# Layer 3's capped mixture: where the fallback, the second biases and the first experts' results are computed

## The reference, cut to what matters

```
probs = softmax(xf @ Wr);  scores, experts = top_k(probs, 2);  scores /= sum
y_fb = gelu(xf @ fw1 + fb1) @ fw2 + fb2          # the fallback, for tokens that overflow
for e in range(8):
    eligible = (token chose e) & ~fb_mask
    rank = cumsum(eligible) - 1
    keep = eligible & (rank < CAP);  overflow = eligible & ~keep
    fb_mask |= overflow
    y = where(overflow, y_fb, y)
    h = gelu(xf[kept tokens] @ W1[e] + b1[e])
    y_e = h @ W2[e] + b2[e]
    y[kept tokens] += y_e * weight
```

## Time and profile before

| | |
|---|---|
| median of 3 runs | 2565.21 us (2561.59 to 2570.26) |
| the profiled execution | 2564.71 us |
| its span | 2562.9 us |
| busy over the span: PE, DVE, ACT, POOL | 78%, 60%, 51%, 19% |
| the last stage | from about 2391 us to the end |

### The profile page before, as it was taken

One profiled execution on the slowest core, in us unless ns is written; L12 is line 12 of the kernel. 1 busy time (PEld: TensorE's weight loads), 2 busy tenths in 40 slices (PEclk: granted clock), 3 DMA queues, 4 the chain that ended last, 5 costly groups with the idle time before them and its releaser, 6 DMA issues.

```text
span 2562.9 us, 40084 instructions
## 1 busy us (share of the span) xinstructions
PE 1999.9 (78%) x14307; PEld 1353.0 (53%) x14307; DVE 1543.1 (60%) x3577; ACT 1306.1 (51%) x2677; POOL 490.2 (19%) x531
## 2 busy tenths in 40 slices
PE   6999757879999999567760678999998984488646
PEld 4666643447777777323440445566665773234435
DVE  6787676756666666457469545666664561478412
ACT  4666434657777776236642146666663120256412
POOL 2111021114232323131025321000100000221133
PEclk9999977989999999769885789999998995689868
DMA  4000004310000000043010000000001010132212
GB/s 172 1 1 2 1 13 90 80 34 1 1 1 1 1 1 1 9 88 86 1 68 0 0 9 1 1 1 1 1 1 77 1 37 13 37 87 60 66 36 68
DMA packets 83302, 73.90 MB, mean 29 GB/s; under 512 B 8633, under 2 KB 76361, under 8 KB 82081
## 3 DMA queue, kind: packets, MB, share of 16 engines
q1 hardware_dynamic: 81313, 68.95, 9.7%
q0 software_dynamic: 1792, 2.38, 0.3%
HBM read 54.73 MB, written 17.62 MB: 28 GB/s over the span
## 4 chain that ended last, share of the span: by engine, by line
PE 49%; DVE 22%; issue 8%; SPq 7%; ACT 7%; another core or an unknown queue 4%; DMA 3%; POOL 1%; DVEq 0%; ACTq 0%; POOLq 0%
PE bank L468 42%; SPq L1408 7%; DMA scratch<-parts 2%; DVE w_keep L1921 1%; PE bank L652 1%; PE bank L2868 1%; PE bank L368 1%; DVE scratch L1225 1%; ACT w_early L3109 1%; PE bank L692 1%; DVE stats L245 1%; DVE w_early L2532 1%; DVE scratch L3007 1%; DVE scratch L720 1%
## 5 line engine op out<-in xcount | busy, mean ns | idle before, releaser
L468 PE MATMUL bank<-scratch 64*128 64x256 bf16 (+5 forms) x3664 | 395.9, 321 | 122.4 <-DMA scratch<-parts 81.7
L468 PEld LDWEIGHTS bank<-scratch 64*128 64x128 bf16 (+3 forms) x3664 | 220.4, 123 | 268.4 <-issue 80.9
L1225 DVE TENSOR_REDUCE scratch<-bank 128x2 f32<-128x512 f32 x384 | 245.9, 687 | 128.1 <-PE bank L468 125.6
L468 PE MATMUL bank<-w_keep,scratch 128*128 128x128 f32 (+4 forms) x1760 | 246.5, 332 | 35.4 <-ACT scratch L805 20.8
L1311 ACT ACTIVATE w_keep<-bank 128x512 f32<-128x512 f32 x384 | 210.4, 596 | 94.9 <-PE bank L468 89.3
L468 PE MATMUL bank<-XNT,w_keep 128*128 128x256 f32 (+4 forms) x800 | 237.6, 436 | 7.2 <-POOL w_keep L2169 2.5
L468 PEld LDWEIGHTS bank<-w_keep,scratch 128*128 128x128 f32 (+3 forms) x1760 | 183.9, 185 | 97.0 <-issue 45.9
L468 PE MATMUL bank<-w_early,scratch 128*128 128x128 f32 (+4 forms) x1184 | 170.8, 350 | 40.2 <-DVE X L3388 24.9
L3109 ACT ACTIVATE w_early<-bank,scratch 128x256 f32<-128x256 f32 x256 | 123.7, 564 | 131.0 <-DVE scratch L3011 131.0
L468 PEld LDWEIGHTS bank<-XNT,w_keep 128*128 128x128 f32 x800 | 149.0, 196 | 60.9 <-issue 29.4
L468 PEld LDWEIGHTS bank<-w_early,scratch 128*128 128x128 f32 (+4 forms) x1184 | 127.6, 191 | 96.4 <-issue 69.0
(11 more groups left out here) (438 smaller groups left out, 3762.9 us busy)
## 6 DMA issues: line engine op xcount, KB each, us to landing
scratch<-parts SPq DMA_DIRECT2D x768, 32.0 KB
parts<-scratch SPq DMA_DIRECT2D x24, 384.0 KB, 2.8
w_early<-pack_l3f SPq DMA_DIRECT2D x1, 4758.0 KB, 14.8
w_keep<-pack_l2f SPq DMA_DIRECT2D x1, 2124.0 KB, 13.3
w_early<-pack_mamba SPq DMA_DIRECT2D x1, 2120.0 KB, 19.1
w_keep<-pack_l2x SPq DMA_DIRECT2D x1, 2049.0 KB, 8.7
w_keep<-taps SPq DMA_DIRECT2D x4, 512.0 KB, 5.4
w_keep<-wave_kernels SPq DMA_DIRECT2D x1, 2048.0 KB
```

The lines of the kernel that those rows point to most:

```text
L468: return pe.matmul(out, lhsT, rhs, start=start, stop=stop, skip_group_check=True)
L1225: dve.tensor_reduce(neg[:, :, h], self.k.bank[5 - g % 2][:, :].rearrange("p (t s) -> p t s", s=S), AXX, ALU.max, negate=True).then_inc(*s. ...
```

## The change: what it does

- The second biases of the experts are packed as rows for all partitions (`z_b2`, 8 x 128 columns), and the instruction that copied an expert's result from the bank now adds its row. `biases_pe`, `turned_act` and `biases_dve` are no longer called in this stage.
- The fallback's bias becomes a product of one row (ones times the bias) in the same bank, a fifth product for each tile; the 16 DVE instructions of L3663 go.
- The second products of fallback jobs 0 and 1 are cut into four pieces each, one behind each expert's rank products. Jobs 2 and 3 follow right behind the ranks: both first products, then both second ones. ACT's order follows.
- DVE's fallback sums move behind the results of experts 1 to 4.
- The semaphore of results is split: experts 0 to 6, and expert 7. SP fetches all of the first half once 0 to 6 are written, then the second half once 7 is; DVE adds all four quarters of the first half, then those of the second.

The diff, without the declarations of the semaphores and the packing:

```diff
@@ def cap_pe(pe):
+        pieces = [piece for job in range(2) for piece in [fallback_down_pe(pe, job)] * 4]
         for e in range(E8):
...
             mm(pe, bank[:, 0:NT], after, el, False, True).then_inc(*s.projected.up("rank", e))
+            next(pieces[e])
@@ def fallback_down_pe(pe, job):
         for j in range(4):
+            o = bank[:, j * P:(j + 1) * P]
             for c in range(C):
-                m = mm(pe, bank[:, j * P:(j + 1) * P], hidden[job % 2][:, c * BANK + j * P:c * BANK + (j + 1) * P],
-                       w["z_fw2"][:, c * D:(c + 1) * D], c == 0, c == C - 1)
-        m.then_inc(*s.summed.up("down", job))
+                mm(pe, o, hidden[job % 2][:, c * BANK + j * P:c * BANK + (j + 1) * P], w["z_fw2"][:, c * D:(c + 1) * D], c == 0, False)
+            m = mm(pe, o, w["ones"][0:1, :], w["z_fb2_bc"][0:1, :], False, True)
+            if j == 3:
+                m.then_inc(*s.summed.up("down", job))
+            yield
@@ def pe(e):
         cap_pe(e)
-        fallback_down_pe(e, 0)
-        fallback_down_pe(e, 1)
-        core.biases_pe(e)
+        core.up_pe(e, 2)
+        core.up_pe(e, 3)
         for job in (2, 3):
-            core.up_pe(e, job)
-            fallback_down_pe(e, job)
+            for _ in fallback_down_pe(e, job):
+                pass
         slots_pe(e, 0)
@@ def result_dve(dve, e):
-        dve.tensor_copy(ys[e], k.bank[6 + e % 2][:, 0:SLOTS]).then_inc(*s.divided.up("expert", e))
+        dve.tensor_tensor(ys[e].rearrange("p (b d) -> p b d", d=D), k.bank[6 + e % 2][:, 0:SLOTS].rearrange("p (b d) -> p b d", d=D),
+                          b2(e).unsqueeze(1).to_broadcast([P, 3, D]), ALU.add).then_inc(*s.divided.up("expert", e))
@@ def dve(e):
         shares_dve(e)
-        core.biases_dve(e)
-        fallback_dve(e)
         turned_dve_(e, 0)
...
             result_dve(e, n)
+            if n <= QUARTERS:
+                fallback_dve(e, n - 1)
         e.wait_ge(*s.vector.at("share", 1, "sum"))
-        for q in range(QUARTERS):
-            for n in range(2):
...
+        for n in range(2):
+            for q in range(QUARTERS):
+                result_sums_dve(e, n, q)
@@ def act(e):
         lower_act(e, 1)
-        core.turned_act(e)
         for job in (2, 3):
             core.raise_act(e, job)
+        for job in (2, 3):
             lower_act(e, job)
@@ def sync(e):
-        e.wait_ge(*s.results_out.at("block", E8 - 1, len(BLOCKS) - 1))
-        for q in range(QUARTERS):
-            for n in range(2):
+        for n in range(2):
+            e.wait_ge(*s.results_out[n].at("block", E8 - 2 + n, len(BLOCKS) - 1))
+            for q in range(QUARTERS):
```

More of the change, by code:

```diff
@@ L3258, in __init__ @@
         self.order, self.top = tmp(k, E8), tmp(k, NT)
-        self.wt = tmp(k, T)
+        self.wt = tmp(k, T) if b2 is not None else None
     def on_dve(self, c):
@@ L3499, in capped_mixture @@
     fallback = [(w["z_fw1"], w["z_fb1"], w["z_fw2"], None)]
-    core = Mixture(k, fallback, MOE3_H, ACT.Gelu, w["z_wr"], w["z_b2"], ALU.max, 1, True)
+    core = Mixture(k, fallback, MOE3_H, ACT.Gelu, w["z_wr"], None, ALU.max, 1, True)
     hidden = core.hidden
@@ L3549, in slots_pe @@
         pe.wait_ge(*s.slots_in[e].at("rows"))
-        pe.wait_ge(*(s.flip_v.at("slots", e - 2) if e >= 2 else s.added.at("b2", e + 2)))
+        pe.wait_ge(*(s.flip_v.at("slots", e - 2) if e >= 2 else s.vector.at("rank", E8 - 1)))
         for b, (at, n) in enumerate(BLOCKS):
@@ L3658, in shares_dve, with fallback_dve, result_sums_dve @@
             dve.tensor_reduce(share[n], same, AXX, ALU.add).then_inc(*up("sum"))
[L3660 to L3665, removed]
-        for q in range(QUARTERS):
-            dve.wait_ge(*s.lowered.at("fallback", q))
-            for i in range(4 * q, 4 * q + 4):
-                o = dve.scalar_tensor_tensor(out=k.X[:, i, :], in0=away[:, i, :], scalar=lost[:, i:i + 1], in1=k.X[:, i, :], op0=ALU.mult, op1=ALU.add)
-            o.then_inc(*s.added.up("fallback", q))
+    def fallback_dve(dve, q):
+        dve.wait_ge(*s.lowered.at("fallback", q))
+        for i in range(4 * q, 4 * q + 4):
+            o = dve.scalar_tensor_tensor(out=k.X[:, i, :], in0=away[:, i, :], scalar=lost[:, i:i + 1], in1=k.X[:, i, :], op0=ALU.mult, op1=ALU.add)
+        o.then_inc(*s.added.up("fallback", q))
+    def result_sums_dve(dve, n, q):
+        dve.wait_ge(*s.fetched_in[n][q].at("rows"))
+        dve.wait_ge(*(s.added.at("result", 0, q) if n else s.added.at("fallback", q)))
+        for i in range(4 * q, 4 * q + 4):
+            o = dve.scalar_tensor_tensor(out=k.X[:, i, :], in0=fetched[n][:, i, :], scalar=share[n][:, i:i + 1], in1=k.X[:, i, :],
+                                         op0=ALU.mult, op1=ALU.add)
+        o.then_inc(*s.added.up("result", n, q))
     def turned_dve_(dve, e):
@@ L4156 @@
     vals.update(z_wr=g[a + "Wr"], z_w1=g[a + "W1"].transpose(1, 0, 2).reshape(P, -1), z_b1=col(g[a + "b1"].ravel()),
-                z_w2=np.concatenate([chunks(w) for w in g[a + "W2"]], 1), z_b2=g[a + "b2"], z_fw1=g[a + "fw1"],
+                z_w2=np.concatenate([chunks(w) for w in g[a + "W2"]], 1), z_b2=rep(g[a + "b2"].ravel()), z_fw1=g[a + "fw1"],
                 z_fb1=col(g[a + "fb1"]), z_fw2=chunks(g[a + "fw2"]), z_fb2_bc=rep(g[a + "fb2"]))
```

16 lines of the change are left out of this document (5 added, 11 removed).

## The result

The changed kernel takes 2547.85 us (median of 10 runs, 2538.43 to 2559.52), the kernel before 2565.18 beside it (10 runs, 2556.31 to 2570.26): ratio 0.9937, 95% interval 0.9914 to 0.9959. The forecast of 2534 was too low by 13.9 us, and 2547 was the upper end of its range. Of the predicted 31.1 us the two profiled executions show 20.2 (2564.71 to 2544.55).

A forecast was written before the change was run, and what follows sets the result against it. The prediction took fallback and bias products to hold up expert 1 some 30 us after POOL delivered its rows. 28.1 us there plus 3 in the tail made 31.1 off 2564.7: 2533.6, median 2534, range 2528 to 2547.

The forecast's parts named there:

- the one on expert 0: Expert 0, 8.4 us long, ends at 2461, hidden 10 us ahead of expert 1's rows.
- the late release stays and takes expert 0: Rival, chance 0.22: under POOL's token writes DVE gets expert 0's turned slots late; +1 to +7 us, forecast 2540.
- the cold clock's 1.7: Expert 1's eight products on PE take 4.11 us, not 2.42, after idling: 1.7 us off the gain.
- The rank loop: Pieces between PE's rank products lengthen the period from 1.13 to 1.29 us; POOL's first token write 1.1 us later.
- the rival of the lower clock: Rival, chance 0.10: PE's ranks run at the lower clock, costing 10.9 us for 1.1; 2544.
- Jobs 2 and 3: These fallback jobs follow the ranks, take 17 us, end at about 2441, hidden under POOL's writes with 10 us spare.
- The tail: Final sums: first results fetched and added ahead; 3.8 us by the steps, bounds 0 to 4.7, taken as 3.
- the sharing: In the final fetches, early fetch and POOL's last rows delay each other; one us less for it.
- The addition in the copy: DVE's copy of each expert's result also adds the second bias: +0, between -0.1 and +0.13 us each.
- The slower rival: Rival, chance 0.04: POOL's indirect writes stall the new additions in experts 1 to 7's results; +57 us, 2590.
- The weighed rule: DVE's fallback sums, with two SBUF inputs, could be held up to 3.8 us each by POOL's result writes; 2535.
- the middle of the change: Expert 1's first product starts 29.8 us earlier, at 2472.3 for 2502.08; 28.1 us left after the clock term.

The follow-up runs named there:

- before_again: The kernel before, unchanged, profiled anew on chip 11: 2542.0 us.
- bias_on_dve: Changed kernel without the one-row products, the fallback's bias again as 16 DVE instructions ahead of the first slots: 2548.86 us (one run).
- half_writes: Changed kernel without POOL's second 16 token writes, SP waiting for the first 16 alone: 2531.85 us (one run).
- half_third: Changed kernel without POOL's second 16 token writes, on chip 6: 2528.33 us (one run).
- half_again: Changed kernel without POOL's second 16 token writes, on chip 5: 2521.1 us (one run).
- wide_pack: Kernel before with the second biases' part of the pack 896 columns wider, never read, on chip 10: 2568.74 us, ratio 1.002.
- lean_again: Changed kernel with fallback jobs 0 and 1 uncut behind the ranks and the fallback's bias as 16 DVE instructions, chip 10: 2554.27 us (one run).
- tail_only: Kernel before with only the results' semaphore split and the first half fetched and added ahead: 2534.53 us, ratio 0.999.
- after_again: The changed kernel, unchanged, run again on chip 11: 2545.55 us, ratio to before 1.001.

## Why the prediction was wrong

*The step that failed is the one on expert 0* ("hidden too, 10 us ahead of expert 1's rows"). It took PE's handoffs during POOL's token writes to be prompt once the bias products are gone. The rival "the late release stays and takes expert 0" describes what happened, down to the place: release at 2475.13 with SP's seven reads (2471.70 on), expert 0 from 2475.18 to the first product of expert 1 at 2484.82. It was priced at +1 to +7; with SP's seven reads from 2471.70, 3.6 to landing and 1.1 for turning, that product could have started at 2476.4, so it came 8.4 late, less the cold clock's 1.7 that expert 0 pays again: 6.7 us. The evidence for it stood in the earlier trace rows: an engine other than DVE, with a finished bank, late in that same stretch. I gave the rival 0.22 because the handoffs of the earlier trace rows behind 2502 were prompt; those stand beside bursts of three writes and not beside 32 in a row.

*A reading of the earlier trace rows* was wrong besides: engines do work in the first of its two pieces. PE goes on there, with gaps, until its first bias products end at 2440.8, 15.2 of the 28.00 us, and POOL writes all along; what idles is DVE. The late release is the other 12.8, and part of the 15.2 is the hold too: these products end 16.4 us behind POOL's first write here and 9.4 in `before_again`.

*The rank loop*: predicted 1.29 us a period, measured 1.55. POOL's first write is 3.0 us later for it, not 1.1: 2.7 in the loop itself, the rest between the logits and the first rank product. The clock was 1.00, as forecast, and the rival of the lower clock did not come. The mis-sized term is the one-row product, costed at 0.24 like two full records and measured at 0.41; by `bias_on_dve` the eight others cost nothing.

*The logits* were 2.3 us later behind the stage's start (13.3 for 11.0; the clock of the stretch behind them is 0.81 for the 1.00 of the earlier trace rows). `half_writes` and `half_third` have it, `half_again`, the same kernel, doesn't, and `wide_pack` has it with before's order: scatter, which no step had.

The three make 6.7 + 1.9 + 2.3 = 10.9, less 0.2 by which the tail was better than forecast: 10.7 of the 10.9 us missing in the profiles (31.1 - 20.2). The other 3 us between the forecast and the median are the profiled run's distance from it (2544.55 to 2547.85).

*Jobs 2 and 3* were to be over by 2441; PE was dense until 2443.7 and then held to 2467. The second product of job 2 took 5.9 us (2434.82 to 2440.72) and not 4.8, again by the one-row products. Neither cost anything by itself: in `lean_again` PE had turned the slots by 2469.1, and DVE got them at 2485.21, behind the writes all the same.

*The tail*: 3.0 forecast, 3.2 measured in the pair and in `tail_only`. It was less than the 3.8 of the steps, and the reason given, the sharing, fits: the second fetch is issued 3.2 us behind the last write's end (2529.48 to 2532.65), 1.24 before, and DVE idles 1.26 us between the halves.

*The addition in the copy*: +0, and 0.56 us like the copy. The slower rival is out: no result waited for POOL. What came late was DVE's plain copy of the slots, and ACT's copies.

*The weighed rule* (two SBUF inputs on DVE are blocked by a GpSimd instruction that reads SBUF): beside POOL's result writes four fallback sums took 1.13 us, as they did alone (1.14 in before). So DVE was not held, as the weighed reading had it; it was POOL: the first write beside them took 1.12 us and not 0.97, and in `before_again` a token write beside the 16 additions L3663, with two SBUF inputs each, took 2.58 (beside the four L3388, with one, the writes took 0.97):

```profile
2446.17 2.58 POOL L3758 DMA_INDIRECT sent<-scratch  x1 [0.30 <-issue]
```

The Trainium skill (SBUF — State Buffer, "Who interferes with whom") speaks of an exclusive lock between the two; the trace agrees as to which instructions meet, with 1.6 us on one write. That is why the 32 writes take 41.7 us there and 39.9 in `after_again`, which has no such additions, or in before under the hold, where they come when the writes are over. It doesn't bear on the hold, in which DVE and ACT wait for PE.

*The condition that no rival had*: where, or when, the program runs. Without the hold the middle of the change, 28.1 of the 31.1 us, does not exist, since the time that it removes is not there.

## What to carry to other kernels

When the profile shows engines waiting behind work that had long ended ("remote", or an empty piece in the chain), find what runs beside it all that time, and cost the next consumer in that stretch as held too, whichever engine it is: removing the instruction that waited moves the wait to the next one. Run the kernel before on another chip before explaining 25 us of it, and compare the stage's own landmarks (here the logits) before calling two stages equal. And give small products their own price: one of a single row between full ones cost 0.41 us here, where a full fp32 one of 128 columns cost 0.24.

## What the runs showed of the hardware

The same kernel took 2540 us on three chips and 2565 on chip 10 and in the first pair. The last stage accounts for it (142.4 for 170.1; 166.0 in `wide_pack`), by the stretch in which POOL issues 32 indirect writes, one each 1.28 us. With the hold PE first runs on for 14 us (19 in `lean_again`; in before ACT's copies of finished transposes come late, by 0.8 us, from 9 us on), then mostly starts one instruction each 0.7 to 2.8 us, and the others see its finished banks late (a product that ended at 2443.6 was added at 2469.70), until 5.1 to 5.6 us behind the start of the last write. It happened as well when the writes moved no rows (one run), and in no trace beside three writes in 5.7 us. What in the chip does it stays open, as does whether it belongs to the chip or to the time, and whether spacing or halving the writes would end it.
